# Attention scores built with keys on the partitions, and row maxima entering as a 65th contraction row

## The chip, the core and the metric

One core of one Trainium2 chip runs the whole kernel. The metric is device time in microseconds (us) of one execution; several runs are made and the median is told. The engines are PE (TensorE, matrix products; PEld are its weight loads), DVE (VectorE), ACT (ScalarE), POOL (GpSimd) and SP (SyncE, which here only issues DMAs). Each engine works through its own queue in order; semaphores order the engines among each other. The profile is of one execution.

## The reference

A transformer block on x of shape (4, 2048, 256): causal attention with 4 heads of 64 and rotary embedding, a residual sum and a layer norm; then a mixture of experts with routing, and a second norm. The change lies in the attention alone:

```python
q, k = (_rope(q), _rope(k))
energy = jnp.einsum('bhtd,bhld->bhtl', q, k) + mask
attn = jax.nn.softmax(energy, axis=-1)
out = jnp.einsum('bhtl,bhld->bhtd', attn, v)
out = out.transpose(0, 2, 1, 3).reshape(B, T, D)
return out @ wo.T
```

`mask` is 0 on and below the diagonal and minus infinity above it. q, k and v are x times three 256 x 256 weights; q and k are scaled by 64 to the power -1/4 each.

## The kernel before

`attention` makes normed rows x1 and the first layer of the router (`hidden`) for 64 tiles of 128 tokens (4 sequences of 16 tiles). Three stages follow it and are the same in both kernels: `route`, `experts`, `last_norm`. They start one after the other, each behind a barrier.

Products that need accuracy are made from an upper part (rounded to the type f32r) and a lower part (the rest). For q and k these are in one contraction: `k_st` holds the upper part of k in partitions 0 to 63 and the lower part in 64 to 127, and `q_parts` holds the upper part of q twice and the lower part of q twice, so that two products make one score. Probabilities and v are multiplied as plain f32, which PE issues as two instructions a product.

A *unit* is one tile of 128 queries and one head (256 units); its keys come in *chunks* of up to 512 (640 chunks). For a chunk:

- PE makes the scores with queries on the partitions (L443, two products, and on the diagonal a mask product, L446) into one of 4 banks;
- DVE takes the maximum over the keys (L744, and L748 over a unit's chunks);
- ACT makes exp(score - maximum) and its sum over the keys (L616);
- PE turns the probabilities in blocks of 128 x 128 (L460), so that keys stand on the partitions;
- DVE or ACT copies the turned block (L758, L625; `chunk_owner` says which);
- PE multiplies it with v (L478) into the one bank `out_ps`, which DVE divides by the sums when the tile's four heads are through (L781).

`FIRST` = 20 tiles are projected (L370), rotated (`rope_products` L906, `rope_sums` L912 and L913, on DVE) and turned (L382) ahead of the loop over chunks. The other 44 are projected inside it, four heads at a time, and rotated on POOL. `attention_slots` writes the order out: a list of steps for each chunk number g. Behind a finished tile come its post steps in nine `ROUNDS`, spread over the chunks of the tile after it: turn of the output (`ot`, L509), output projection (`wo`), residual and norm (`ln`, `x1` L809, with one power on POOL, `rstd`, L887), statistics for the router (`stats`, with another power on POOL, L892), turn of x1 (`x1t`, L521) and `hidden` for each second tile. All engines walk the same list (`walk`). `tile_order` puts the short tiles of one sequence between the long ones of the next, and the last sequence's short tiles at the end. On SP's queue stand the loads of x_t (for a tile's projection) and of x rows, and the stores of x1 and of hidden columns.

Of the kernel before, what the change touches and what calls it, by code (L numbers as in the profile page):

```python
# [7 lines left out]
P = 128  # L8
HEADS = 4
HD = 64  # L10
D = 256
# [41 lines left out]
ONE = 1  # L53

AHEAD = 4
PROBS_RING = 8
PT_RING = 4
CH = 512


def raw(ap):
# [4 lines left out]
ROUNDS = (  # L66
    (("qt", 1),),
    (("qt_read", 1), ("kt", 1)),
    (("kt_read", 1), ("proj", 0)),
    (("proj_read", 0), ("ot", 1), ("v", 1)),  # L70
    (("v_read", 1), ("ot_read", 1), ("rope", 0), ("x1t", 2)),
    (("x1t_read", 2), ("wo", 1), ("hidden", 2)),
    (("hidden_read", 2), ("wo_read", 1), ("ln", 1), ("xt", -1)),
    (("x1", 1),),
    (("stats", 1), ("dup", 0)),
)
PROJECTION = ("qt", "kt", "proj", "v", "rope", "xt", "dup")


def tile_order(NB, NT):  # L80

    order = []
    for b in range(NB):
        long = list(reversed(range(4, NT)))
        fill = [(b - 1, t) for t in (3, 2, 1, 0)] if b else []
        for n, t in enumerate(long):
            if n < len(fill):
                order.append(fill[n])
            order.append((b, t))
            if b == NB - 1 and 4 <= n < 8:  # L90
                order.append((b, 7 - n))
    return order


def attention_slots(NB, NT):

    order = tile_order(NB, NT)
    count = len(order)
    units = [(m, h) for m in range(count) for h in range(HEADS)]
    banks = [order[m][1] // 4 + 1 for m, _ in units]  # L100
    chunks = [(u, c) for u, n in enumerate(banks) for c in range(n)]
    start = [sum(banks[:HEADS * m]) for m in range(count + 1)]
    total = len(chunks)

    products, done = [[] for _ in range(total + 2)], 0
    for g in range(total + 2):
        behind = 1 if g >= total or chunks[g][1] in (0, banks[chunks[g][0]] - 1) else 2
        while done < min(g + 1 - behind, total):
            products[g].append(done)
            done += 1  # L110

    span = [(start[m], start[m + 1]) for m in range(count)] + [(total, total + 2)] * 2
    m = 0
    while m < count - 1:
        if order[m][1] < 4 <= order[m + 1][1]:
            half = (start[m] + start[m + 2]) // 2
            span[m], span[m + 1] = (start[m], half), (half, start[m + 2])
            m += 1
        m += 1

    projected = NT + 4
    early, late = ([[] for _ in range(total + 3)] for _ in range(2))
    at, made = 0, {}
    late[0].append(("xt", projected))
    for s in range(count + 2):
        lo, hi = span[s]
        if 1 <= s <= count:
            early[start[s]].append(("sums", s - 1))
            late[start[s]].append(("norm", s - 1))
        for r, steps in enumerate(ROUNDS):  # L130
            offset = r * (hi - lo - 1) // (len(ROUNDS) - 1)
            if r < 3 and s < count and order[s][1] == 3 and order[s][0] < NB - 1:
                offset = 0
            at = min(max(at, lo + offset), total + 2)
            for k, back in steps:
                of = s - back
                if k.removesuffix("_read") in PROJECTION:
                    of += projected
                    if not projected <= of < NB * NT:
                        continue  # L140
                elif not 0 <= of < count:
                    continue
                if k.endswith("_read") and made[k[:-5], of] < at:
                    early[at].append((k, of))
                else:
                    made[k, of] = at
                    late[at].append((k, of))

    for m in range(2, count):
        late[start[m - 1] - 2].append(("q_split", m))  # L150
    return order, units, chunks, banks, products, early, late


def attention(nc, dram, NB, NT):

    order, units, chunks, banks, products_at, early, late = attention_slots(NB, NT)
    CHUNKS = len(chunks)
    first_chunk = np.concatenate([[0], np.cumsum(banks)]).tolist()
    COUNT = NB * NT
    FIRST = NT + 4  # L160
    assert FIRST % 2 == 0 and COUNT % 4 == 0

    def slot(b, t):

        return NT + t if t < 4 and b % 2 else t

    projected = [(n // NT, n % NT) if n < FIRST else
                 (order[n - FIRST][0] + (2 if order[n - FIRST][1] < 4 else 1), order[n - FIRST][1])
                 for n in range(COUNT)]
    nth_projected = {bt: n for n, bt in enumerate(projected)}  # L170
    assert len(nth_projected) == COUNT and max(b for b, _ in projected) == NB - 1

    def cols(b, t):
        return slice(slot(b, t) * P, (slot(b, t) + 1) * P)
# [23 lines left out]
    def walk(main, step):  # L198

        for g in range(len(late)):  # L200
            for kind, k in early[g]:
                step(kind, k)
# [1606 lines left out]
```

## Time and profile before

| | us |
|---|---|
| median of 3 runs | 2280.97 (2280.77 to 2282.14) |
| span of the profiled execution | 2278.6 |
| attention: start to the last product with v | 0 to 1449 |
| post steps of the last tile | 1449 to 1469.5 |
| route, experts, last norm | 1469.5 to 2278.6 |

| engine | busy us | share of the span | instructions |
|---|---|---|---|
| PE | 1967.0 | 86% | 14370 |
| PEld | 1800.5 | 79% | 14370 |
| DVE | 1453.1 | 64% | 3388 |
| ACT | 1361.2 | 60% | 3413 |
| POOL | 805.8 | 35% | 891 |

The span runs from the first to the last instruction on the chip; the page gives no time of its own for this execution, so the span stands beside the median of the runs. PE's busy time counts matmuls that overlap only once, but a matmul's own duration includes its way through the array; what one more matmul costs is therefore read from the start of one to the start of the next. A share of the whole span mixes stages with different limits, so the rows below are taken by stage.

### The profile page before, as it was taken

The numbers are of one execution on the slowest core, as the hardware profiler recorded it, in microseconds if no ns is written. First come the engines' busy times: TensorE is split into PE (matmuls) and PEld (weight loads), VectorE is DVE, ScalarE is ACT, GpSimd is POOL, SyncE is SP. The second block draws the span as 40 slices with busy tenths as digits, with TensorE's granted clock in tenths as the row PEclk, the third lists the DMA queues.
The fourth block names the chain that finished last, engine by engine and source line by source line (L and its number), as shares of the span: only waits on it lengthen the run. The fifth ranks groups of instructions, "written<-read, shape, count | busy, mean of one in ns | idle before, by whom it ended". The sixth has DMA issues, their size and how long they took to land. (4 is left out here: it accounts for less than half of the span.)

```text
span 2278.6 us, 43372 instructions
## 1 busy us (share of the span) xinstructions
PE 1967.0 (86%) x14370; PEld 1800.5 (79%) x14370; DVE 1453.1 (64%) x3388; ACT 1361.2 (60%) x3413; POOL 805.8 (35%) x891
## 2 busy tenths in 40 slices
PE   7899999999999999999999998552177999999990
PEld 6799988888888888888888887451177999999980
DVE  7655676565666666666666676376794566556645
ACT  6666665666666666666566654315175666666655
POOL 2222333323233333233111111100085667666642
PEclk9899999999999999999999999655588999999995
DMA  2000011010001100010000000220004444554428
GB/s 69 21 11 22 22 32 34 22 31 29 27 22 33 32 25 29 23 32 29 20 31 27 24 29 31 78 86 1 0 1 127 148 138 144 162 169 128 149 51 295
DMA packets 91409, 135.85 MB, mean 60 GB/s; under 512 B 16932, under 2 KB 79376, under 8 KB 87148
## 3 DMA queue, kind: packets, MB, share of 16 engines
q1 hardware_dynamic: 75372, 123.52, 15.8%
q0 software_dynamic: 15872, 10.24, 2.7%
q8 instruction: 91, 1.49, 0.3%
q14 instruction: 74, 0.61, 0.1%
HBM read 104.62 MB, written 39.85 MB: 63 GB/s over the span
## 5 line engine op out<-in xcount | busy, mean ns | idle before, releaser
L478 PE MATMUL out_ps<-v_sb,probs_t 128*128 128x64 f32 x4352 | 549.4, 271 | 17.7 <-DVE attn L781 15.2
L478 PEld LDWEIGHTS out_ps<-v_sb,probs_t 128*128 128x128 f32 x4352 | 530.6, 193 | 27.2 <-DVE probs_t L758 20.5
L744 DVE TENSOR_REDUCE part_max<-scores_ps 128x1 f32<-128x512 f32 (+3 forms) x576 | 356.8, 621 | 202.7 <-PE scores_ps L443 148.1
L616 ACT ACTIVATE probs<-scores_ps,neg_max 128x512 f32<-128x512 f32 (+3 forms) x640 | 397.6, 627 | 44.4 <-DVE neg_max L748 42.3
L443 PE MATMUL scores_ps<-k_st,q_parts 128*128 128x512 f32 (+3 forms) x1280 | 410.5, 403 | 11.3 <-ACT probs L616 4.9
L625 ACT COPY probs_t<-probs_t_ps 128x512 f32<-128x512 f32 (+3 forms) x416 | 208.2, 501 | 244.8 <-PE probs_t_ps L460 243.5
L460 PE MATMUL probs_t_ps<-ident,probs 128*128 128x128 f32 x2176 | 347.1, 275 | 1.0 <-DVE probs_t L758 1.0
L460 PEld LDWEIGHTS probs_t_ps<-ident,probs 128*128 128x128 f32 x2176 | 261.4, 142 | 51.2 <-issue 2.4
L1519 PE MATMUL up_ps<-xe_t,w 128*128 128x320 f32 x1920 | 289.2, 310 | 2.2 <-DVE xe_t L1626 1.7
L1519 PEld LDWEIGHTS up_ps<-xe_t,w 128*128 128x128 f32 x1920 | 283.8, 189 | 2.9 <-issue 1.9
L443 PEld LDWEIGHTS scores_ps<-k_st,q_parts 128*128 128x128 f32 x1280 | 200.5, 193 | 25.2 <-ACT probs L616 7.2
L887 POOL TENSOR_TENSOR rstd<-mean_var,power 128x1 f32<-128x1 f32 x64 | 35.6, 556 | 480.0 <-DVE mean_var L801 480.0
L906 POOL TENSOR_TENSOR products<-qk,cos_sin 128x256 f32<-128x256 f32 x176 | 125.4, 744 | 218.3 <-ACT qk L556 218.3
L1640 DVE SCALAR_TENSOR_TENSOR h<-silu,up_ps 128x320 f32<-128x320 f32 x160 | 77.1, 482 | 182.8 <-ACT silu L1596 182.8
L1482 POOL DMA_INDIRECT acc_rows<-out_rows,token x96 | 148.7, 1548 | 127.2 <-ACT out_rows L1609 116.3
L1519 PE MATMUL y_ps<-w,h_parts 128*128 128x256 f32 x1440 | 181.0, 285 | 0.0
L1519 PEld LDWEIGHTS y_ps<-w,h_parts 128*128 128x128 f32 x1440 | 174.4, 191 | 2.2
L1621 DVE TENSOR_TENSOR w<-w_raw,w 128x768 fp32r<-128x768 f32 x160 | 153.0, 958 | 5.0 <-ACT w L1574 1.3
L758 DVE COPY probs_t<-probs_t_ps 128x512 f32<-128x512 f32 (+1 forms) x224 | 145.9, 651 | 0.7 <-PE probs_t_ps L460 0.6
L1462 POOL DMA_INDIRECT rows<-x_rows,token_in x96 | 128.9, 1343 | 48.0 <-POOL token_in L1459 28.4
L1574 ACT CAST w<-w_raw 128x768 fp32r<-128x768 f32 x160 | 131.7, 825 | 8.1 <-PEq L940 8.1
L616 ACT ACTIVATION_READ_ACCUMULATOR probs<-scores_ps,neg_max 128x1 f32 x640 | 130.4, 204 | 0.0
(234 smaller groups left out, 3038.8 us busy)
## 6 DMA issues: line engine op xcount, KB each, us to landing
w_raw<-in_w_expert SPq DMA_DIRECT2D x32, 1536.0 KB
w_raw<-in_w_adapter SPq DMA_DIRECT2D x32, 384.0 KB
x_t<-in_x_t SPq DMA_DIRECT2D x64, 128.0 KB, 2.1
x_row<-in_x SPq DMA_DIRECT2D x64, 128.0 KB, 2.0
x_rows<-x SPq DMA_DIRECT2D x64, 128.0 KB, 1.7
acc_rows<-x SPq DMA_DIRECT2D x64, 128.0 KB, 1.8
ln_x<-acc_rows SPq DMA_DIRECT2D x16, 512.0 KB, 6.3
out_rows_dram<-ln_y SPq DMA_DIRECT2D x16, 512.0 KB, 5.2
```

The source lines that it names most:

```text
L443: mm = pe.matmul(out, q_parts[:, m % 2, part_, h, :], k_st[:, h, key_cols(g)], start=part_ == 0, stop=part_ == 1 and not diagonal)
L460: mm = pe.transpose(t_ps[:, g % 2, a:a + P], probs[:, g % PROBS_RING, a:a + P], ident[:])
L478: mm = pe.matmul(o_ps[:, h, :], probs_t[:, g % PT_RING, a - lo:a - lo + P], v_sb[:, slot(b, a // P), h, :], start=a == 0, stop=a == t * P)
L616: act.activation(probs[:, g % PROBS_RING, 0:hi - lo], s_ps[:, g % AHEAD, 0:hi - lo], ACT.Exp, bias=neg_max[:, u % 8:u % 8 + 1], accum_out= ...
L625: act.copy(probs_t[:, g % PT_RING, 0:hi - lo], t_ps[:, g % 2, 0:hi - lo]).then_inc(probs_copied[1], 1)
L744: red = dve.tensor_reduce(neg_max[:, ring:ring + 1] if single else part_max[:, ring, c:c + 1], s_ps[:, g % AHEAD, 0:hi - lo], AX.X, ALU.ma ...
L758: dve.tensor_copy(probs_t[:, g % PT_RING, 0:hi - lo], t_ps[:, g % 2, 0:hi - lo])\
L1462: pool.indirect_dma_start(out=rows[0:n, r, t, :], out_offset=None, in_=dram["x1"], in_offset=bass.IndirectOffsetOnAxis(ap=token_in[0:n, r, ...
L1482: pool.indirect_dma_start(out=dram["acc"], out_offset=bass.IndirectOffsetOnAxis(ap=token[0:n, r, t:t + 1], axis=0), in_=out[0:n, r, t, :], ...
L1519: mm = pe.matmul(o, left(a), right(b), start=start and n == 0, stop=stop and n == 2)
L1574: act.copy(columns(w[:, r, 0], p), columns(w_raw[:, r], p)).then_inc(w_upper, 1)
L1621: dve.tensor_tensor(columns(w[:, r, 1], p), columns(w_raw[:, r], p), columns(raw(w[:, r, 0]), p), ALU.subtract).then_inc(w_split, 1)
```

## The change

Sequences are worked one after the other, and each in two *phases* of two heads. A unit is now one *group* of four query tiles (512 queries) and one head (64 units), and a chunk is 128 keys against these 512 queries (640 chunks, as before).

- Scores come out with keys on the partitions: the stationary operand is a block of k, the moving one the group's queries (L470, L471). exp of them is the stationary operand of the product with v as it stands (L486), so turns and copies of probabilities are gone.
- The maximum of a query is now needed before the score is built. It is taken from a product of its own, with queries on the partitions and without the lower part of q (L451, one product of up to 512 keys for a query tile; the mask L454; DVE L683). The negative maxima of a unit are turned by PE into a row (L440, four turns of 65 x 128) and copied by DVE into partition 64 of `q_low`, while partition 64 of `k_one` holds ones: the second score product contracts 65 rows, 64 of lower q against upper k and one that subtracts the maximum.
- v has a 65th column of ones, so that the products with v give the sums too (65 columns). `out_ps` has two banks; scores of either kind have two.
- A projection is of two heads (384 columns, L386). 12 of the 128 are made ahead of the loop.
- `Plan` replaces `attention_slots`: one slot for each chunk and 25 more. The post steps of a tile come 8, 5 or 4 slots after those of the tile before it; those of tiles 60 to 63 lie behind the last chunk. The upper half of k is copied once more (`again_k`, POOL).

The core of the diff, with the new order:

```diff
-AHEAD = 4
-PROBS_RING = 8
-PT_RING = 4
...
 CH = 512
+FIRST = 12
+S_AHEAD = 2
+P_RING = 4
...
+class Plan:
...
+        self.groups = [(f, G) for f in range(PH) for G in range(NG)]
+        self.units = [(y, hh) for y in range(len(self.groups)) for hh in range(2)]
+        self.size = [4 * self.groups[y][1] + 4 for y, _ in self.units]
...
+                pace = 8 if self.start[u + 1] < total - per else 5 if self.start[u + 1] < total else 4
+                at = max(at + pace if post else 0, self.start[u + 1] + 1)
...
+            base = 3 * (n - FIRST) if f == 0 else 12 + 4 * t if f == 1 else per * (f - 1) + 5 * t
...
+            late[base].append(("proj", n))
+            early[base + 1].append(("proj_read", n))
+            late[base + 6].append(("kt", n))
...
+                    cur = min(cur - 1, self.start[u] - 6)
...
+            late[at].append(("ot", m))
+            early[at + 1].append(("ot_read", m))
+            late[at + 2].append(("wo", m))
+            early[at + 3].append(("wo_read", m))
+            early[at + 3].append(("ln", m))
+            early[at + 4].append(("x1", m))
+            late[at + 4].append(("stats", m))
+            late[at + 6].append(("x1t", m))
+            early[at + 7].append(("x1t_read", m))
+            late[at + 7].append(("hidden", m))
...
         @block.tensor
...
-                for part_ in range(2):
-                    mm = pe.matmul(out, q_parts[:, m % 2, part_, h, :], k_st[:, h, key_cols(g)],
-                                   start=part_ == 0, stop=part_ == 1 and not diagonal)
...
+            def score(e):
...
+                at_least(pe, score_read, e - 1)
+                if c is None:
+                    pe.wait_ge(neg_ready, u + 1)
+                    for t in range(4):
+                        mm = pe.transpose(out[0:HD + 1, cols(t)], neg_pad[:, u % 2, t, :], ident[:])
...
+                    return
...
+                mm = pe.matmul(out[:, 0:n], q_two[:, ring, hh, cols(i)], k_st[:, h, c * CH:c * CH + n],
+                               start=True, stop=not diagonal)
...
+            def ahead(g):
...
+                at_least(pe, exp_done, g - 1)
+                pe.matmul(out, k_st[:, h, cols(kb)], q_two[:, ring, hh, i * P:CH], start=True, stop=False)
+                mm = pe.matmul(out, k_one[:, h, cols(kb)], q_low[:, ring, hh, i * P:CH], start=False, stop=not diagonal)
...
-                    mm = pe.transpose(t_ps[:, g % 2, a:a + P], probs[:, g % PROBS_RING, a:a + P], ident[:])
...
+                    mm = pe.matmul(o_ps[:, u % 2, t * OS:t * OS + HD + 1], probs[:, g % P_RING, cols(t)],
+                                   v_sb[:, kb, h, 0:HD + 1], start=kb == 0 and t == 0, stop=kb == 4 * G + t,
...
         @block.scalar
...
-                               bias=neg_max[:, u % 8:u % 8 + 1], accum_out=sums[:, m % 2, h, c:c + 1])\
...
+                act.activation(probs[:, g % P_RING, i * P:CH], s_ps[:, g % 2, i * P:CH], ACT.Exp).then_inc(exp_done, 1)
...
         @block.vector
...
+                    dve.tensor_copy(q_low[HD:HD + 1, ring, hh, :], x_ps[HD:HD + 1, e % 2, :]).then_inc(score_read, 1)
...
+                n = (i + 1) * P if c == G else CH
+                dve.tensor_reduce(part_max[:, u % 4, i, c:c + 1], x_ps[:, e % 2, 0:n], AX.X, ALU.max).then_inc(score_read, 1)
+                if e == plan.last_entry[u]:
...
+                    dve.tensor_reduce(neg_pad[:, u % 2, :, HD], part_max[:, u % 4, :, 0:G + 1], AX.X, ALU.max,
+                                      negate=True).then_inc(neg_ready, 1)
```

How the order moves shows at three places. First, PE's queue in the middle of the loop. Before, with `probs_t_ps` the turned probabilities and `out_ps` the products with v (a "128x64" is a product):

```order
L443 MATMUL scores_ps<-k_st,q_parts 128x512 x2
L460 MATMUL probs_t_ps<-ident,probs 128x128 x4
L478 MATMUL out_ps<-v_sb,probs_t 128x64 x8
L443 MATMUL scores_ps<-k_st,q_parts 128x512 x2
L460 MATMUL probs_t_ps<-ident,probs 128x128 x4
```

and now, with `scores_t_ps` the scores with keys on the partitions, `scores_ps` the product for the maxima and `proj_ps` the turned k of a half tile:

```order
L470 MATMUL scores_t_ps<-q_two,k_st 128x512
L471 MATMUL scores_t_ps<-q_low,k_one 128x512
L486 MATMUL out_ps<-v_sb,probs 128x65 x4
L451 MATMUL scores_ps<-k_st,q_two 128x512
L400 MATMUL proj_ps<-ident,k_rows 128x128 x2
```

The four turns of a chunk went, and one product of 512 columns came.

Second, POOL's queue around a post step's power `rstd`. Before:

```order
L906 TENSOR_TENSOR products<-qk,cos_sin 128x256 x4
L912 TENSOR_TENSOR roped<-products 128x8x32
L913 TENSOR_TENSOR roped<-products 128x8x32
L887 TENSOR_TENSOR rstd<-mean_var,power 128x1
L857 TENSOR_TENSOR x_t_parts<-x_t,x_t_parts 128x256
L866 TENSOR_TENSOR q_parts<-q_t,q_parts 128x512
L892 TENSOR_TENSOR x<-powers_of,power 128x2
```

and now, in one alignment of projections and posts (`x<-powers_of` is the second power):

```order
L833 TENSOR_TENSOR products<-qk,cos_sin 128x128 x4
L842 TENSOR_TENSOR q_rows<-products 128x128
L843 TENSOR_TENSOR q_rows<-products 128x128
L842 TENSOR_TENSOR k_rows<-products 128x128
L843 TENSOR_TENSOR k_rows<-products 128x128
L788 COPY k_one<-k_st 64x2x128
L818 TENSOR_TENSOR rstd<-mean_var,power 128x1
L783 TENSOR_TENSOR x_t_parts<-x_t,x_t_parts 128x256
L823 TENSOR_TENSOR x<-powers_of,power 128x2
L833 TENSOR_TENSOR products<-qk,cos_sin 128x128 x4
```

A half tile's rope is eight operations instead of six, and comes every four or five slots; where a post's power falls against it changes from post to post.

Third, the end of PE's queue in this stage, from the last product with v on. Before:

```order
L478 MATMUL out_ps<-v_sb,probs_t 128x64 x5
L509 MATMUL misc_ps<-ident,attn 128x128 x2
L521 MATMUL misc_ps<-ident,x 128x128 x2
L522 MATMUL misc_ps<-ident,x 6x128
L370 MATMUL misc_ps<-w_o,attn_t 128x256 x6
L521 MATMUL misc_ps<-ident,x 128x128 x2
L522 MATMUL misc_ps<-ident,x 6x128
L370 MATMUL misc_ps<-x_t,w_r 128x256 x6
L370 MATMUL misc_ps<-x_ts,w_r1s 128x256 x3
```

and now, the first seven rows:

```order
L486 MATMUL out_ps<-v_sb,probs 128x65 x6
L516 MATMUL misc_ps<-ident,attn 128x128 x2
L386 MATMUL misc_ps<-w_o,attn_t 128x256 x6
L516 MATMUL misc_ps<-ident,attn 128x128 x2
L530 MATMUL misc_ps<-ident,x 128x128 x2
L531 MATMUL misc_ps<-ident,x 6x128
L386 MATMUL misc_ps<-w_o,attn_t 128x256 x6
```

One `ot` (`ident,attn`) stood behind the last product with v, and now there are four.

## Rows read from the trace of the kernel before

**Rows 1.** Busy time by stage; (x) counts instructions, PEclk is the granted clock

```profile
95.00:1400.00 1305.00, 1252.83 (x9599) 1125.05 (x9599) 830.93 (x2135) 831.97 (x2355) 372.06 (x489) 0.99 0.09 27
1400.00:1449.00 49.00, 42.77 (x305) 39.13 (x305) 31.58 (x89) 21.56 (x72) 4.31 (x6) 0.90 0.07 21
```

**Rows 2.** Timeline, PE in steady attention: start us, duration us, instruction

```profile
1003.55 0.62 PE L443 MATMUL scores_ps<-k_st,q_parts 128*128 128x512 f32 x2
1004.01 0.60 PE L460 MATMUL probs_t_ps<-ident,probs 128*128 128x128 f32 x4
1004.45 0.33 PE L478 MATMUL out_ps<-v_sb,probs_t 128*128 128x64 f32 x2
...
1004.85 0.23 PE L446 MATMUL scores_ps<-causal,ident_b 128*128 128x128 bf16 x1
1004.91 0.61 PE L460 MATMUL probs_t_ps<-ident,probs 128*128 128x128 f32 x4
...
1005.50 0.96 PE L370 MATMUL misc_ps<-w_qkv,x_t_parts 128*128 128x256 f32 x6
1006.29 0.63 PE L443 MATMUL scores_ps<-k_st,q_parts 128*128 128x512 f32 x2
```

**Rows 3.** Groups of instructions by line: busy us, mean ns, idle before

```profile
L478 PE MATMUL out_ps<-v_sb,probs_t 128*128 128x64 f32 x4352 | 549.4, 271 | 17.7 <-DVE attn L781 15.2 <-DVE probs_t L758 1.9
...
L744 DVE TENSOR_REDUCE part_max<-scores_ps 128x1 f32<-128x512 f32 x432 | 296.6, 687 | 172.4 <-PE scores_ps L443 148.1 <-PE scores_ps L446 14.1
...
L906 POOL TENSOR_TENSOR products<-qk,cos_sin 128x256 f32<-128x256 f32 x176 | 125.4, 744 | 218.3 <-ACT qk L556 218.3
```

**Rows 4.** Timeline, DVE during the first tiles

```profile
11.95 1.43 DVE L906 TENSOR_TENSOR products<-qk,cos_sin 128x256 f32<-128x256 f32 x4 [0.30 <-ACT qk L592]
...
22.50 1.43 DVE L906 TENSOR_TENSOR products<-qk,cos_sin 128x256 f32<-128x256 f32 x4 [0.34 <-ACT qk L556]
24.02 0.79 DVE L912 TENSOR_TENSOR roped<-products 128x256 f32<-128x256 f32 x1
24.73 0.41 DVE L913 TENSOR_TENSOR roped<-products 128x256 f32<-128x256 f32 x1
25.18 0.69 DVE L717 TENSOR_TENSOR k_st<-probs_t_ps,k_st 64x512 f32 x1
26.17 1.43 DVE L906 TENSOR_TENSOR products<-qk,cos_sin 128x256 f32<-128x256 f32 x4 [0.30 <-ACT qk L556]
```

**Rows 5.** Timeline, PE where the main loop starts

```profile
94.91 1.22 PE L443 MATMUL scores_ps<-k_st,q_parts 128*128 128x512 f32 x2 [1.83 <-ACT probs L616]
```

**Rows 6.** Instructions of L912, ns minimum/median/maximum

```profile
L912 DVE TENSOR_TENSOR roped<-products x20: 425/789/793, 13.5 to 83.2; 128x256 f32<-128x256 f32 x20
```

**Rows 7.** Waits of PE and its weight loads: us, times, longest

```profile
PE out_ps L478 <- DVE attn L781: 15.2, 16, 2.4
...
PEld out_ps L478 <- DVE probs_t L758: 20.5, 26, 2.5
```

**Rows 8.** Timeline, PE after the last attention product

```profile
1447.65 1.33 PE L478 MATMUL out_ps<-v_sb,probs_t 128*128 128x64 f32 x10 [1.15 <-DVE probs_t L758]
1451.05 0.66 PE L509 MATMUL misc_ps<-ident,attn 128*128 128x128 f32 x2 [2.08 <-DVE attn L781]
1452.63 0.69 PE L521 MATMUL misc_ps<-ident,x 128*128 128x128 f32 x2 [0.92 <-DVE attn_t L785]
...
1454.78 1.65 PE L370 MATMUL misc_ps<-w_o,attn_t 128*128 128x256 f32 x6 [1.25 <-DVE x_ts L832]
1461.88 0.66 PE L521 MATMUL misc_ps<-ident,x 128*128 128x128 f32 x2 [5.45 <-POOL x L892]
...
1464.00 1.65 PE L370 MATMUL misc_ps<-x_t,w_r 128*128 128x256 f32 x6 [1.25 <-DVE x_ts L832]
```

**Rows 9.** Timeline, other engines in the same stretch, and the route stage

```profile
1458.57 0.41 DVE L809 TENSOR_SCALAR x<-y,mean_var,rstd 128x256 f32<-128x256 f32 x1 [0.67 <-POOL rstd L887]
...
1469.51 0.20 POOL L1043 MEMSET ident<- 128x128 f32 x1 [7.78 <-POOLq L207]
```

More of the change, by code:

```diff
@@ L77 @@
[L77 to L151, printed above, removed]
@@ L154, in attention @@
-def attention(nc, dram, NB, NT):
[L156 to L174, printed above, removed]
-    owner = [chunk_owner(banks[u], c, u) for u, c in chunks]
-    nth = [owner[:g].count(owner[g]) for g in range(CHUNKS)]
-    copies = [owner.count(e) for e in range(2)]
-    def keys(g):
-        u, c = chunks[g]
-        return c * CH, min((c + 1) * CH, (order[units[u][0]][1] + 1) * P)
-    def key_cols(g):
-        u, c = chunks[g]
-        lo, hi = keys(g)
-        at = slot(order[units[u][0]][0], 4 * c) * P
-        return slice(at, at + hi - lo)
-    def latest_key(g):
-        u, c = chunks[g]
-        b, t = order[units[u][0]]
-        return max(nth_projected[b, x] for x in range(4 * c, min(4 * c + 4, t + 1)))
[L198 to L202, printed above, removed]
-            main(g)
-            for kind, k in late[g]:
-                step(kind, k)
@@ L357, in _ @@
+            for g in range(plan.slots):
+                for kind, k in plan.early[g] + plan.late[g]:
+                    step(kind, k)
             for r in range(2):
@@ L480, in multiply @@
                 mm.then_inc(values_done, 1)
             def main(g):
-                if g + AHEAD < CHUNKS:
-                    scores(g + AHEAD)
+                if g + S_AHEAD < CHUNKS:
+                    ahead(g + S_AHEAD)
                 if g < CHUNKS:
-                    turn(g)
-                for j in products_at[g] if g < CHUNKS + 2 else ():
-                    multiply(j)
+                    multiply(g)
+                for e in plan.score_at[g]:
+                    score(e)
@@ L531, in step @@
                           start=False).then_inc(hid_done, 1)
-            for g in range(AHEAD):
-                scores(g)
-            walk(main, step)
-            while reads:
-                pe.wait_ge(*reads.pop(0))
+            walk(main, step, score, ahead)
+            for bank in pending:
+                pe.wait_ge(*pending[bank])
         @block.scalar
         def _(act):
-            for semaphore in (exp_done, hid_copied, qk_copied, v_copied, q_copied, probs_copied[1]):
-                act.sem_inc(semaphore, ONE)
@@ L877, in step @@
                 elif kind == "proj_read":
[L878 to L884 removed]
+                    pool.wait_ge(qk_copied, k + 1)
@@ L893, in step @@
                         .then_inc(stats_ready, 1)
-            for m in range(2):
-                split_q(m)
-            walk(main, step)
+            walk(nothing, step, nothing, nothing)
 def rope_products(eng, cos_sin, qk, products, t):
```

820 lines of the change are left out of this document (425 added, 395 removed).

## The prediction

> **What bounds the kernel now.** First the busy time by stage [rows 1]: from 95 to 1400 us PE is busy 1252.8 of 1305 us at a granted clock of 0.99, DVE 831, ACT 832, POOL 372. So attention, about 60% of the span, goes by PE's queue. PE's own timeline says what an instruction is worth there, read from start to start, since matmuls overlap [rows 2]: two 512-wide score products 0.46 us (1003.55 to 1004.01), so 0.235 each; four turns of probabilities 0.44, so 0.11 each; a mask 0.06; six 256-wide projection products 0.79, so 0.13 each. Two further stages belong to the change: the first tiles, which end where the main loop's first score starts, at 94.91 [rows 5], and the time from the last attention product (1447.65 + 1.33 = 1448.98) to the start of the route stage at 1469.51 [rows 8, 9]. After that nothing is edited. The sum is made against the profiled execution, span 2278.6; the median of the three runs lies 2.4 above, and I add that at the end. About 0.2%, 4.6 us, is what a measurement can tell from no change.
>
> **PE's exchange in the main loop.** Out go the 2176 turns of probabilities: 2176 x 0.11 = 239 us. In come, by the counts of the two instruction orders:
> - 640 products for the maxima: 448 of 512 columns at 0.235 = 105, and 64 each of 384, 256 and 128 at about 0.14 = 27;
> - a second mask on the diagonal, 256 x 0.06 = 15;
> - the row of negative maxima, 256 turns x 0.11 = 28;
> - projections. Only 12 half tiles instead of 20 whole ones are made ahead of the loop, so 696 products of 384 columns (taken at 0.18, between 0.13 and 0.235) = 125 replace 264 x (0.235 + 0.13) = 97, and there are 120 more turns of q and k, 13. Together 41;
> - less 24 score products that are made ahead of the loop, about 5.
>
> That is 211 in against 239 out: **-28 us**. The pair of score products and the products with v keep their counts. The latter have 65 columns instead of 64: nothing if the weight load sets their pace, at most 1/64 of 549 = 9 us [rows 3]; I take nothing, because an f32 turn of 128 columns has the same 0.11 with one weight load.
>
> The Trainium skill speaks against the size of this term: "TensorE: Matmul & The Clock Gate", section "Back-to-back issue gap", gives sustained spacings of about 81 ns at 128 columns and 131 ns at 512. By these figures (an estimate) the turns are 176 and the 448 wide maxima 59 us, a margin of 117 instead of the 134 of my figures. The rows differ from both figures, and my sum uses the rows.
>
> **Waits that go.** PE waits 15.2 us for the one output bank to be normalised, and its weight loads 20.5 us for copied probabilities [rows 7]. The output bank becomes two and the copy is gone: -36. The last tiles of the order before are short ones: 305 PE instructions take 49 us, at the rate of the main loop 305/9599 x 1305 = 41.5 [rows 1]. The new order ends with its longest units: -7. Together **-43 us**.
>
> **Waits that come.** Maxima now have two score banks, so PE may be two slots (about 2 us each) ahead of DVE. DVE loses the copies of probabilities and gains 64 one-partition row copies and the lower part of q; its 0.69 us maxima stay [rows 3], so it stays near its 64% of this stage and is no bound by itself. What is queued behind what matters more. POOL's rope has eight 128-wide operations per half tile; between half of a 256-wide one and the whole (0.37 to 0.74 [rows 3]) I take 0.5, so 4.0 us every four or five slots. A post step's two powers stand in that queue. When rstd comes right behind a rope (one alignment in five), DVE has x1 up to 3.4 us late; two score banks cover that, but the statistics follow and PE's turn of x1 comes some 1.6 us too early: 64 x 0.3 = 19. Each unit's row needs PE's four turns and a DVE copy of about 0.7 us one slot before its first product: cost between nothing and the whole 1.4, I take 0.3 as DVE has a slot's slack: 19. In the first phase projections come every three slots against some 5.5 us of POOL work: 7. Together **+45 us**, bounds 0 and 64 x (1.6 + 1.4) = 192.
>
> **The first tiles.** DVE sets their pace: 26.17 - 22.50 = 3.67 us a tile, of which its operations fill 1.43 + 0.79 + 0.41 + 0.69 = 3.3 [rows 4]. A half tile has eight rope operations of half the width instead of six. Purely by width a half tile is 1.84 us, by number 3.67; I take 3.0, so 12 take 36 from the same 11.95. Then come setting of the ones row (4096 values in one partition), eight q tiles to turn (1.2 each) and 24 maxima at up to 0.69 with their three rows: 28. The loop starts at 11.95 + 36 + 28 = 76 instead of 94.91: **-19 us** (bounds -41 and -4).
>
> Here a row bears on DVE and POOL working side by side: the rope sums of L912 took 0.425 at the least and 0.789 in the median [rows 6], 0.36 more, where POOL was splitting the next x. I have one such delay in the 3.0. The Trainium skill, "SBUF — State Buffer", section "Who interferes with whom", says that a VectorE instruction with two SBUF inputs and a GpSimd one that reads SBUF lock one port pair, and the loser waits for the whole instruction. That is a rival below.
>
> **The end.** The old order leaves one tile's post work after the last product with v; the new one leaves four (tiles 60 to 63 need both heads of the last unit), four slots apart with nothing between. The old tail shows each link [rows 8, 9]. Last product to the turn of attn 2.07; to PE's next step, which waits for attn's split, 1.58; output projection to x1 1454.78 to 1458.57 = 3.79. So x1 of the first is out 7.4 after the last product. The next one's projection waits in PE's queue behind this one's turn of x1 (3.31 after x1) and its split (1461.88 to 1464.00 = 2.12), so the period is 3.31 + 2.12 + 3.79 = 9.2. Three periods, then x1 to the route stage 10.94: 7.4 + 27.7 + 10.9 = 46 against 20.5 now: **+26 us**.
>
> **At no cost.** ACT loses the accumulator reads and its copies of probabilities and gains smaller reads; it is 64% busy in the loop and exp has two slots of lead. x_t is loaded 128 times instead of 64, each two projections (at least six slots) ahead on SP's queue; x rows, stores and hidden columns follow the plan's slots there, behind signals that are due by then. If that cover went, each late load would cost PE its 2 us or so.
>
> **Sum.** -28 - 43 + 45 - 19 + 26 = -19: 2259.6 for the profile, with 2.4 on it **2262 us**, a ratio of 0.992. Its own range, from the bounds of the start and half the bounds of the waits, is 2235 to 2276.
>
> **Rivals.**
> 1. **Posts wait in POOL's queue, and PE with them** (slower). DVE stands at x1 while rstd is behind rope; maxima stand behind DVE; PE reaches its third maximum, or the turn of x1, and stops. For: POOL goes from 372 to some 690 us of this stage, with rope right ahead of rstd in its order. Against: two slots of lead, and DVE idle for a third of the time. Price: if every post loses the 1.6 that I gave to the worst alignment, 64 x 1.6 = 102 in place of 19: 2345 us. It decides from 0.6 us a post on.
> 2. **The waits are hidden** (faster still). All chains fit in their two slots: the 45 goes, 2217 us. For it speaks that plan slots are two steps apart for each step of a chain; against it, that the old order has 36 us of waits of just this kind.
> 3. **The port** (no change). If the loser waits a whole POOL instruction of 0.73 at both POOL operations of a half tile, the start is 12 x (1.46 - 0.36) = 13 longer, and x1 of every fifth post reaches PE later by as much, some 4: 2279 us. For: 0.789 against 0.425. Against: the 0.36 is half an instruction.
>
> **How the numbers follow.** My forecast 0.42, rival 1 0.29, rival 2 0.22, rival 3 0.07. Faster is the forecast and rival 2, 0.64; no change rival 3, 0.07; slower rival 1, 0.29. The range 2200 to 2335 takes in rival 2 with room for a quicker start, and rival 1 up to 1.4 us a post; the rest of rival 1, about a tenth, is left out above, and somewhat less below.
>
> **What would show it.** The main loop's first score at about 76; 640 products for the maxima at a start-to-start of 0.235; the time from there to the last product with v near 1328 us (1354 - 28 - 43 + 45); POOL about half busy there; rstd waiting on POOL in one post of five; 46 us from the last product to the route stage. Wrong would be: PE waiting hundreds of times for a score bank or for DVE's row; a products-with-v group that grew by more than 9 us; a start later than 91; a lower granted clock in the loop.

## The result, and the profile after

The change makes the kernel slower: median 2341.19 us of 4 runs (2327.95 to 2351.55) against 2280.87 for the kernel before, a ratio of 1.026 (95% interval 1.023 to 1.029). The forecast was 2262, the range 2200 to 2335. Runs differ with the mean granted clock: the shortest of the changed kernel, 2328 us, had 0.888, its two longest, 2350.5 and 2351.6, had 0.878 and 0.879, and one run of e9 below, at 0.633, took 2737 us against 2197 to 2199 for its other five. The profiled execution is one of the long ones, with a span of 2348.7.

First the busy time by stage, for the kernel before and after, from the main loop's start (its first score before, its first product with v after) to the last product with v. Columns: stretch, its length, busy time and instructions of PE, PEld, DVE, ACT and POOL, granted clock, DMA share, GB/s.

Before:

```profile
94.90:1449.00 1354.10, 1295.69 (x9904) 1164.28 (x9904) 862.51 (x2223) 853.63 (x2427) 376.37 (x495) 0.99 0.09 26
```

After, the loop and then the lowest two and the highest of six stretches of 200 us in it, which answer to [rows 1]:

```profile
83.80:1494.60 1410.80, 1353.86 (x9085) 1215.09 (x9084) 801.67 (x2003) 610.06 (x1610) 593.75 (x1278) 0.93 0.10 31
...
200.00:400.00 200.00, 193.62 (x1260) 174.31 (x1260) 110.24 (x270) 85.00 (x223) 87.84 (x191) 0.89 0.10 29
...
800.00:1000.00 200.00, 194.36 (x1335) 174.70 (x1334) 117.41 (x289) 89.56 (x238) 95.24 (x206) 0.95 0.11 32
...
1200.00:1400.00 200.00, 193.01 (x1241) 172.20 (x1240) 112.75 (x286) 82.54 (x213) 64.25 (x137) 0.88 0.09 27
```

PE has 819 instructions fewer in the loop and is busy 58 us longer. Its pauses, the time in which it is not busy, are the same in sum: 1354.1 - 1295.7 = 58 us before, 1410.8 - 1353.9 = 57 after. But 28 of them are over a microsecond now, 39.9 us together, and 12 were before, 19.9 us. The other difference is the clock column: 0.99 before, 0.93 after, and in the stretches 0.88 to 0.95. By the clock's own record in the trace, 207 us of this loop ran at 1.2 GHz, the lower of its two levels, against 32 us before. At half the clock PE does about half the work (an instruction of the products with v takes 200 ns from start to start in those stretches, and 103 ns at the higher level), so about half of that time is lost: 103 us against 16. So **some 87 us** of the loop are the clock. Without pauses and without that half, PE's work is 1354.1 - 58.4 - 15.9 = 1280 us before and 1410.8 - 56.9 - 103.3 = 1251 after. That the exchange of work did save PE some 29 us can be read here and nowhere in the total.

Where does the clock fall? One case in the changed kernel: the timelines of DVE and POOL and then of PE (start us, duration us, instruction, and in brackets the idle time before it and who ended that), and the busy time by stretch around it.

```profile
320.53 0.18 DVE L730 BATCH_NORM_AGGREGATE mean_var<-moments 128x2 f32<-128x6 f32 x1
320.79 0.15 DVE L732 TENSOR_SCALAR mean_var<-mean_var 128x1 f32<-128x1 f32 x1
...
321.06 0.46 POOL L842 TENSOR_TENSOR q_rows<-products 128x128 f32<-128x128 f32 x1
...
322.30 0.46 POOL L843 TENSOR_TENSOR k_rows<-products 128x128 f32<-128x128 f32 x1
...
322.72 0.55 POOL L818 TENSOR_TENSOR rstd<-mean_var,power 128x1 f32<-128x1 f32 x1
```

```profile
324.00 0.48 PE L451 MATMUL scores_ps<-k_st,q_two 128*128 128x512 f32 x1
324.31 0.40 PE L470 MATMUL scores_t_ps<-q_two,k_st 128*128 128x512 f32 x1
324.55 0.39 PE L471 MATMUL scores_t_ps<-q_low,k_one 65*128 65x512 f32 x1
324.78 1.00 PE L486 MATMUL out_ps<-v_sb,probs 128*128 128x65 f32 x8
...
327.26 0.41 PE L530 MATMUL misc_ps<-ident,x 128*128 128x128 f32 x2 [1.29 <-POOL x L823]
```

```profile
310.00:325.00 15.00, 15.00 (x109) 13.83 (x107) 10.13 (x25) 7.50 (x21) 9.43 (x21) 1.00 0.07 19
325.00:328.00 3.00, 1.71 (x15) 1.53 (x14) 1.98 (x8) 1.08 (x4) 1.38 (x2) 1.00 0.00 0
328.00:340.00 12.00, 12.00 (x48) 10.44 (x47) 2.45 (x6) 3.36 (x10) 3.80 (x9) 0.50 0.14 44
340.00:355.00 15.00, 15.00 (x63) 13.80 (x63) 6.77 (x18) 3.22 (x10) 1.31 (x3) 0.50 0.12 36
355.00:370.00 15.00, 15.00 (x106) 13.85 (x104) 9.41 (x21) 8.20 (x21) 10.14 (x22) 0.99 0.07 19
```

`mean_var` is ready at 320.94; `rstd` stands behind a rope in POOL's queue until 322.72, 1.8 us later. x1 is late by it, and PE pauses 1.29 us at its turn of x1 (L530). At 328 the clock falls to half and stays there for 27 us, in which PE never waits: 48 matmuls in 12 us at half the clock, 106 in 15 us after it. Each of the 15 falls in this loop comes 1.3 to 3.5 us after the beginning of such a pause, of 1.15 to 2.03 us; a stretch at half clock lasts 3 to 27 us. The other 13 pauses over a microsecond brought no fall, and the length of a pause does not set what it costs: the six of 1.29 or 1.30 us at L530 were followed by 20 to 27 us at half clock each, 143 in all, and the three of 2.02 or 2.03 us there by none, 3 and 7.

The waits of PE from 90 to 1495 us (us in all, times, longest):

```profile
PE misc_ps L530 <- POOL x L823: 19.8, 20, 2.0
PE proj_ps L400 <- POOL k_rows L843: 13.1, 9, 1.7
PE misc_ps L530 <- DVE attn_t L719: 6.0, 8, 1.2
PE scores_ps L451 <- DVE part_max L683: 3.7, 4, 1.2
PE proj_ps L386 <- DVE k_st L652: 3.0, 3, 1.0
PE scores_ps L451 <- DVE q_low L680: 2.8, 5, 0.6
```

Two kinds of pause are the longest, L530 and L400. The second is named after the wrong engine. The timeline at one of them:

```profile
284.83 0.15 DVE L756 TENSOR_SCALAR powers_of<-x 128x1 f32<-128x1 f32 x1
285.02 0.43 DVE L652 TENSOR_TENSOR k_st<-proj_ps,k_st 64x256 fp32r<-64x256 f32 x1
...
285.50 0.20 PEld L400 LDWEIGHTS proj_ps<-ident,q_rows 128*128 128x128 f32 x2 [1.96 <-DVE k_st L652]
285.50 0.44 PE L400 MATMUL proj_ps<-ident,q_rows 128*128 128x128 f32 x2 [1.66 <-POOL k_rows L843]
```

PE wants to turn q into the bank `proj_ps`, where the k turned one slot earlier still waits for DVE: the lower part of k (L652) stood behind the six statistics of a post step. POOL's `k_rows` ended by chance at the same time; the weight load's row has the right name.

### The profile page after: what moved, and what is told of

Its sections match the earlier page's. It is cut to its first block and busy times, and to the rows that moved or that the text cites. A ratio compares the mean times of both kernels' runs of the same rounds, so it can differ in the third digit from the quotient of the medians.

```text
span 2348.7 us, 40554 instructions
## 1 busy us (share of the span) xinstructions
PE 2013.2 (86%) x13346; PEld 1833.9 (78%) x13346; DVE 1393.7 (59%) x3208; ACT 1084.1 (46%) x2549; POOL 1022.5 (44%) x1683
## 5 line engine op out<-in xcount | busy, mean ns | idle before, releaser
L486 PEld LDWEIGHTS out_ps<-v_sb,probs 128*128 128x128 f32 x4352 | 607.6, 204 | 35.9
L683 DVE TENSOR_REDUCE part_max<-scores_ps 128x1 f32<-128x512 f32 (+3 forms) x640 | 388.5, 609 | 388.8 <-PE scores_ps L454 231.2
L486 PE MATMUL out_ps<-v_sb,probs 128*128 128x65 f32 x4352 | 605.1, 281 | 0.0
L582 ACT ACTIVATE probs<-scores_t_ps 128x512 f32<-128x512 f32 (+3 forms) x640 | 340.9, 533 | 324.1 <-PE scores_t_ps L473 183.7
L833 POOL TENSOR_TENSOR products<-qk,cos_sin 128x128 f32<-128x128 f32 x464 | 199.9, 461 | 382.6 <-ACT qk L559 342.4
L451 PE MATMUL scores_ps<-k_st,q_two 128*128 128x512 f32 (+3 forms) x640 | 298.1, 468 | 9.8 <-DVE part_max L683 4.3
L470 PE MATMUL scores_t_ps<-q_two,k_st 128*128 128x512 f32 (+3 forms) x640 | 272.5, 426 | 0.0
L471 PE MATMUL scores_t_ps<-q_low,k_one 65*128 65x512 f32 (+3 forms) x640 | 245.1, 383 | 0.0
L386 PE MATMUL proj_ps<-w_qkv,x_t_parts 128*128 128x384 f32 x696 | 158.7, 367 | 3.8 <-DVE k_st L652 3.0
L451 PEld LDWEIGHTS scores_ps<-k_st,q_two 128*128 128x128 f32 x640 | 130.7, 205 | 16.7 <-DVE part_max L683 8.4
L386 PEld LDWEIGHTS proj_ps<-w_qkv,x_t_parts 128*128 128x128 f32 x696 | 133.8, 206 | 8.8 <-DVE k_st L652 3.7
```

The costliest lines, as they stand in the source:

```text
L386: mm = pe.matmul(out, parts_l(a), parts_r(b), start=start and n == 0, stop=stop and n == 2)
L451: mm = pe.matmul(out[:, 0:n], q_two[:, ring, hh, cols(i)], k_st[:, h, c * CH:c * CH + n], start=True, stop=not diagonal)
L470: pe.matmul(out, k_st[:, h, cols(kb)], q_two[:, ring, hh, i * P:CH], start=True, stop=False)
L471: mm = pe.matmul(out, k_one[:, h, cols(kb)], q_low[:, ring, hh, i * P:CH], start=False, stop=not diagonal)
L486: mm = pe.matmul(o_ps[:, u % 2, t * OS:t * OS + HD + 1], probs[:, g % P_RING, cols(t)], v_sb[:, kb, h, 0:HD + 1], start=kb == 0 and t == 0 ...
L582: act.activation(probs[:, g % P_RING, i * P:CH], s_ps[:, g % 2, i * P:CH], ACT.Exp).then_inc(exp_done, 1)
```

## The experiments

Theory A: PE's pauses of over a microsecond are what the falls of the clock follow, so they cost several times their length. Rival B: waits cost only themselves, and the clock goes its own way. Theory C: the product for the maxima is dearer than I took it, for its place ahead of two other f32r products. Each run was timed against the kernel before on the same chip. The columns on the right are of the profiled execution: the loop's length (first to last product with v; before, from the loop's first score), PE's pauses in it, time at half clock in it, and length - pauses - half of the half-clock time. Counted from its first product with v too, the kernel before has 1349.7, 58, 27 and 1278.

| kernel | median us | ratio to before, 95% | span | loop | pauses | half clock | rest |
|---|---|---|---|---|---|---|---|
| before | 2280.9 | | 2278.6 | 1354.1 | 58 | 32 | 1280 |
| the change | 2341.2 | 1.023 to 1.029 | 2348.7 | 1410.8 | 57 | 207 | 1251 |
| e1_rope_after | 2256.7 | 0.987 to 0.990 | 2255.5 | 1316.4 | 41 | 28 | 1262 |
| e2_rope_before | 2406.9 | 1.053 to 1.060 | 2396.0 | 1458.8 | 112 | 181 | 1256 |
| e3_kt_later | 2295.2 | 1.002 to 1.008 | 2280.3 | 1343.0 | 67 | 28 | 1262 |
| e4_between | 2266.4 | 0.992 to 0.995 | 2263.8 | 1326.4 | 49 | 56 | 1249 |
| e5_filler | 2276.8 | 0.997 to 1.001 | 2304.5 | 1364.8 | 43 | 102 | 1271 |
| e6_lag | 2235.2 | 0.979 to 0.983 | 2231.2 | 1293.8 | 32 | 6 | 1259 |
| e7_lag_between | 2230.8 | 0.976 to 0.985 | 2216.2 | 1280.0 | 27 | 4 | 1251 |
| e8_tail | 2213.1 | 0.969 to 0.978 | 2211.6 | 1283.8 | 27 | 11 | 1251 |
| e9_xt_early | 2197.9 | 0.963 to 0.965 | 2195.4 | 1267.0 | 17 | 5 | 1248 |
| e10_half_maxima | 2172.3 | 0.951 to 0.954 | 2169.1 | 1242.4 | 29 | 4 | 1212 |

The last column is 1248 to 1262 us for every kernel that does just the work of the change (e5 does 141 instructions more, and e10 leaves out some). Pauses and clock are the rest.

**Order on POOL.** Projections every fourth slot instead of every fifth keep a fixed place to the posts, which come every eighth. With + 1 each rope stands behind a post's two powers:

```diff
-ROW_RING = 12
+ROW_RING = 16
-            base = 3 * (n - FIRST) if f == 0 else 12 + 4 * t if f == 1 else per * (f - 1) + 5 * t
+            base = 3 * (n - FIRST) if f == 0 else 12 + 4 * t if f == 1 else per * (f - 1) + 4 * t + 1
...
```

> Projections every fourth slot, placed so that POOL's rope always stands behind a post step's two powers; 16 row buffers instead of 12, nothing else. Theory A (a pause of PE of more than about a microsecond is followed by a stretch at half clock): the 19.8 us of PE waiting at its turn of x1 fall below 5, the half-clock time in the loop falls from about 200 us to below 90, and the time from 2341 to about 2341 - 18 - 55 = 2268. Rival B (the clock goes its own way, waits cost only themselves): half-clock time stays near 200 us and the time falls by the waits alone, to about 2322.

Measured 2256.7, 84 us less than the change and 24 less than before. In the loop the waits at the turn of x1 are 11.6 us instead of 19.8 (up to 1.5 each; more than the 5 expected), the half-clock time 28 us instead of 207. This speaks for theory A; rival B's 2322 is 65 us off. The waits at L400 went as well, from 16.1 us by all that ended them to 1.5, so the turn of x1 is not all that the new order eased.

With + 3 in place of + 1, and nothing else changed against e1, a rope stands right ahead of `rstd`:

```diff
-            base = 3 * (n - FIRST) if f == 0 else 12 + 4 * t if f == 1 else per * (f - 1) + 4 * t + 1
+            base = 3 * (n - FIRST) if f == 0 else 12 + 4 * t if f == 1 else per * (f - 1) + 4 * t + 3
```

> The same kernel as the one with rope behind the powers, but with projections two slots later, so that a rope always stands right ahead of rstd in POOL's queue. Theory A: nearly every post with rope beside it makes PE wait about a microsecond at its turn of x1, some 50 us in all, and half-clock time in the loop grows to over 300 us: 2341 + 30 + 50 = about 2420. Rival B: the waits alone, about 2370, and the half-clock time as before.

Measured 2406.9: nearly A's time, but not in A's way. The waits of PE from 84 to 1543 us:

```profile
PE proj_ps L400 <- DVE k_st L652: 43.4, 16, 4.0
PE proj_ps L386 <- DVE k_st L652: 31.8, 21, 2.1
...
PE misc_ps L530 <- POOL x L823: 8.1, 8, 1.5
```

The late posts show at the bank `proj_ps`, because the lower part of k stands behind them on DVE. Half-clock time did not grow to 300; it is 181 us, in 27 stretches instead of 15, half as long on average, and here B's "as before" was nearer. Against the change 55 us more are pauses (112 - 57) and 13 less the clock. So this run tells that the order on POOL sets the pauses, and not how much clock a pause costs.

**The bank of k and q.**

```diff
-            late[base + 6].append(("kt", n))
-            early[base + 7].append(("kt_read", n))
+            turn = base + (6 if f == 0 else 7 if f == 1 else 8)
+            late[turn].append(("kt", n))
+            early[turn + 1].append(("kt_read", n))
...
```

> PE's turn of k one or two slots later, nothing else. Theory A: the 13.1 us that PE waits for k_rows at L400 go, and with them the six falls of the clock behind such a wait (41 us at half clock): 2341 - 13 - 20 = about 2308. The falls behind the turn of x1 stay. Rival B: -13, about 2328.

Measured 2295.2 (2282 to 2316; the profiled execution is one of the shorter ones), 46 us less where A said 33, and my reading was wrong on two points. What waits at L400 is the turn of q, and for DVE (above). And the pauses did not get less: 67 us, 30 of them over a microsecond, 39.0 us together (28 and 39.9 in the change), yet the clock fell only three times, each behind a pause of 2.44 us, and half of the half-clock time is 14 us instead of 103. The waits at the turn of x1 were left as they were, and here one of 1.25 us passed with no fall (busy time by stretch, this kernel):

```profile
300.00:318.00 18.00, 18.00 (x129) 16.46 (x128) 12.44 (x32) 8.73 (x26) 9.15 (x20) 1.00 0.11 35
318.00:322.00 4.00, 2.75 (x24) 2.50 (x23) 2.98 (x11) 2.09 (x6) 1.73 (x3) 1.00 0.06 17
322.00:340.00 18.00, 17.21 (x123) 15.31 (x123) 10.40 (x26) 7.98 (x22) 7.92 (x18) 1.00 0.18 56
```

So a pause is what a fall follows, but not every pause has one. Which ones do stays open.

**The place of the product for the maxima.**

```diff
                 for t in range(i, 4):
+                    if t > i and rest:
+                        score(rest.pop(0))
...
```

> The product for the maxima is put between two products with v instead of right ahead of the next pair of score products. Theory C (an f32r product of 512 columns takes 0.315 us to the next f32r product but 0.234 to an f32 one): PE saves up to 0.08 us for each of 640 products, 35 to 50 us, about 2298, with the clock as it was. Rival: the 0.08 only moves to another place, 2341 within 8.

Measured 2266.4, 75 us less, but theory C is wrong. PE in that kernel:

```profile
333.97 0.33 PE L489 MATMUL out_ps<-v_sb,probs 128*128 128x65 f32 x2
334.11 0.48 PE L451 MATMUL scores_ps<-k_st,q_two 128*128 128x512 f32 x1
334.43 0.33 PE L489 MATMUL out_ps<-v_sb,probs 128*128 128x65 f32 x2
```

From 334.11 to 334.43 it is 0.32 us, with a plain f32 product behind it, as it was 0.31 ahead of an f32r one (324.00 to 324.31 above). The work of the loop is the same, 1249 against 1251. The loop of the profiled execution is 84 us shorter: 75 is half of the 151 us less at half clock, and 8 are pauses. Why this order, with 25 pauses over a microsecond, has fewer falls (7) stays open as well.

**Useless work in the pauses.** The sharpest test of A leaves every wait in place and fills the twelve longest at the turn of x1:

```diff
+LATE = dict.fromkeys((3, 13, 16, 19, 29, 35, 45, 48, 52), 10) | dict.fromkeys((8, 24, 40), 17)
...
                     claim("b", x1_split, k + 1)
+                    for _ in range(LATE.get(k, 0)):
+                        pe.transpose(b_ps[:, 3 * P:4 * P], ident[:], ident[:])
                     pe.wait_ge(stats_ready, k + 1)
```

> The changed kernel with useless work added: ahead of the twelve turns of x1 at which PE paused over a microsecond, 10 or 17 turns of the identity into a free part of the bank (1.1 or 1.9 us). Nothing arrives earlier, PE's waits are only filled. Theory A (it is PE's pause that the half clock follows): the eight falls behind such a pause, 154 us at half clock, go, and the kernel is faster by up to 77 us for 141 more instructions: about 2270. Rival B (waits cost themselves, the clock goes its own way): 2341 or up to 5 more.

Measured 2276.8: 141 instructions more, and 64 us less, near A's 2270 and far from B's 2341. PE, and the busy time by stretch, at the post shown above:

```profile
325.91 1.26 PE L530 MATMUL misc_ps<-ident 128*128 128x128 f32 x10
327.27 0.44 PE L533 MATMUL misc_ps<-ident,x 128*128 128x128 f32 x2
```

```profile
324.00:328.00 4.00, 3.90 (x31) 3.47 (x31) 3.08 (x10) 2.15 (x7) 1.39 (x2) 1.00 0.00 0
328.00:340.00 12.00, 12.00 (x92) 10.76 (x90) 5.37 (x14) 4.83 (x13) 4.83 (x11) 1.00 0.17 56
340.00:355.00 15.00, 14.52 (x102) 13.26 (x101) 10.72 (x26) 7.76 (x21) 8.18 (x19) 1.00 0.12 36
```

The turn of x1 comes at 327.27 as it came at 327.26, and the clock stays: 92 matmuls from 328 to 340 us instead of 48. All eight falls behind the turn of x1 are gone. Five others remain, each behind a pause of 1.65 to 2.01 us at L400, which was not filled; a sixth came at 1403 behind three pauses of 0.34 to 0.46. The profiled execution, 2306 us, is the longest of this kernel's eleven: there the clock then stayed at half to the end of the loop.

**Taking the pauses away.**

```diff
-            late[at + 6].append(("x1t", m))
-            late[at + 7].append(("hidden", m))
+            late[at + 6 + lag[m]].append(("x1t", m))
+            late[at + 7 + 2 * lag[m]].append(("hidden", m))
...
```

`lag` is 1 for posts eight slots apart, else 0; the reads follow; the rest is as in the kernel with rope behind the powers.

> As the kernel with rope behind the powers, and PE's turn of x1 one slot later, hidden two. If the remaining 27 us of waits at that turn (some 15 in the loop, the rest in the tail) and the three falls behind them (24 us at half clock) cost what they seem to: 2257 - 10 - 12 = about 2235. If the waits only move to hidden or to the next turn of attn: 2257.

Measured 2235.2. No fall in the loop at all, though 15 pauses of over a microsecond are left, 17.5 us together.

> The same with the product for the maxima put between two products with v. Its start-to-start stayed 0.314 us there, so what it brought before was the clock (207 us at half clock before, 56 with it). If that is so, little is left to bring here: 0 to 13 us faster than the kernel without it, 2222 to 2235. If it saves PE time of its own, 40 or more: below 2200.

Measured 2230.8 (2218.0 to 2240.7; the profiled execution is the shortest), which can't be told from e6. With the clock up, the place of the product brings next to nothing, as it should if its gain was the clock.

The last four posts two slots apart:

```diff
-                pace = 8 if self.start[u + 1] < total - per else 5 if self.start[u + 1] < total else 4
+                pace = 8 if self.start[u + 1] < total - per else 5 if self.start[u + 1] < total else 2
```

> The same, and the last four post steps two slots apart instead of four, so that PE makes the next tile's output projection before this one's turn of x1. The tail from the last product with v to the route stage, 45 us, has three periods of 9.2 us; if DVE's chain of about 6.5 us is what is left of a period, 8 us faster than the kernel without it; if steps of neighbouring tiles get in each other's way, the same or slower.

Measured 2213.1 (2210.6 to 2232.5). PE's last products with v and the route stage's first row:

```profile
1366.30 1.50 PE L490 MATMUL out_ps<-v_sb,probs 128*128 128x65 f32 x12
...
1402.34 0.21 POOL L971 MEMSET ident<- 128x128 f32 x1 [7.77 <-POOLq L222]
```

1402.34 - 1367.80 = 34.5 us; e7 and the change both have 44.3 (the change's rows stand below): 10 less in the tail. The medians differ by 18, but the runs of both spread by 22, so the tail's 10 is what the profile shows.

```diff
-                late[max(base - 2, 0)].append(("xt", n))
+                late[max(base - (4 if f > 1 else 2), 0)].append(("xt", n))
```

> As the kernel with the shorter tail, and POOL splits the next x two slots earlier, ahead of the rope that it now stands behind. The 10.8 us in 16 waits of PE for that split go: about 2203 against 2213. If the split, earlier, pushes rope and the powers back by as much as it gains: 2213.

Measured 2197.9: **3.6% faster than the kernel before and 6.1% faster than the change**, with the same arithmetic. Its pauses are 17 us instead of 27 and the wait for the split is gone:

```profile
83.70:1350.70 1267.00, 1249.78 (x9085) 1132.52 (x9084) 790.93 (x2003) 610.18 (x1610) 597.27 (x1278) 1.00 0.11 35
```

**The price of a product for the maxima.**

```diff
-                n = (i + 1) * P if diagonal else CH
+                n = (i + 1) * P if diagonal else CH // 2
...
```

> The kernel with the shorter tail, with 384 of the 640 products for the maxima (those of whole key chunks) over half their keys, and DVE's maxima of them too: half of those chunks is left out of the maximum. If a product for the maxima costs PE what the trace shows from start to start, 0.33 us at 512 columns and 0.21 at 256: 384 x 0.12 = 46 us less, 2167. If it costs the 0.235 and 0.14 of the prediction: 384 x 0.095 = 36 less, 2177. If PE is no longer what bounds the loop: nothing.

Measured 2172.3, 41 less than e8; the loop's rest falls by 39 (1251 to 1212). Halving 384 products took off 0.10 us each, between the 0.095 of my prices and the 0.12 of the trace. Of the full 0.32, then, about 0.1 does not go with the columns.

## Why the prediction was wrong

The stages of the profiled executions add up: 11 us less ahead of the loop, 57 more in it, 24 more behind it and 0.5 in the stages that were not edited are 70, and the spans differ by 2348.7 - 2278.6 = 70. By the prediction's own steps, with the loop's parts summed from the start of one matmul to the start of the next and pauses left out:

- **PE's exchange, -28: right, by misses that nearly cancel.** The rest column gives 1251 - 1280 = -29 (-21 in e6, whose loop is at full clock). In e6 the products for the maxima are 0.33, 0.26, 0.21 and 0.15 us at 512, 384, 256 and 128 columns: 448 x 0.33 + 64 x 0.62 = 188 us instead of 132, 56 too few. The turns that go were 242 (239 taken). On the other side the products with v took 450 us against 464 before although they have 65 columns; the pair of score products 287 against 301 (5 fewer taken), the rows 22 (28 taken), projections of every kind with the turns of q and k 260 against 230 (41 more taken). Together these turn -28 into some -15, 6 short of e6's -21. The margin of turns over wide maxima is 242 - 148 = 94. My rows gave 134. The estimate by the Trainium skill, "TensorE: Matmul & The Clock Gate", section "Back-to-back issue gap", gave 117, nearer, but from 81 and 131 ns, where the traces have 111 and 330.
- **Waits, -43 + 45: right in sum, and partly by luck.** Pauses 58 before, 57 after. The 19 us at the turn of x1 are 19.8, by the mechanism that was named (`rstd` behind rope, PE 1.3 us too early in the post above), but in 20 posts, by 1.0 us on average and 2.0 at most, instead of 1.6 in one post of five. The 19 for the rows were 2.8 and the 7 of the first phase 3.0; not foreseen were 16.1 at L400 (13.1 in the row above for `k_rows`). On the other side, the 20.5 us that were to go with the copies of probabilities are waits of weight loads [rows 7]; PE's own for those copies were 2.9 (1.9 at the products with v, 1.0 at the turns).
- **The first tiles, -19: -12.** The loop's first score stands at 83.13 (76 forecast, 94.91 before [rows 5]). The half tiles came every 2.9 us (12.02 to 44.21 for eleven) as taken (3.0); what follows them, from 47 us on, took 36 instead of 28, with the clock at half from 35 to 89 us. DVE's first and last of the twelve, and PE:

```profile
12.02 1.43 DVE L833 TENSOR_TENSOR products<-qk,cos_sin 128x128 f32<-128x128 f32 x4 [2.86 <-ACT qk L559]
...
44.21 0.90 DVE L833 TENSOR_TENSOR products<-qk,cos_sin 128x128 f32<-128x128 f32 x4
...
83.13 0.56 PE L470 MATMUL scores_t_ps<-q_two,k_st 128*128 128x256 f32 x1
```

- **The end, +26: +24.** From the last product with v (1493.31 + 1.50) to the route stage 44.3 us, 46 forecast, 20.5 before [rows 8, 9], with the period of 9.2 between turns of x1:

```profile
1493.31 1.50 PE L486 MATMUL out_ps<-v_sb,probs 128*128 128x65 f32 x12
...
1503.41 0.66 PE L530 MATMUL misc_ps<-ident,x 128*128 128x128 f32 x2 [4.47 <-POOL x L823]
...
1512.63 0.66 PE L530 MATMUL misc_ps<-ident,x 128*128 128x128 f32 x2 [4.24 <-POOL x L823]
...
1539.10 0.20 POOL L967 MEMSET ident<- 128x128 f32 x1 [7.79 <-POOLq L221]
```

- **The step that failed is one that isn't there: the clock.** Each term was priced at the 0.99 of [rows 1], and the 45 us of new waits at their own length. The pauses have the same sum as before, but 28 instead of 12 are over a microsecond: before, 0.99 of the clock with 58 us of pauses; now 0.93 with 57. That is the missing 87 us: 1328 forecast for the loop plus 87 is 1415, measured 1411. "A lower granted clock in the loop" stood in the list of what would make the prediction wrong, with no price and no chance. Filled pauses (e5), pauses taken away (e1, e6) and the sum in the last column show that it is the cause. Which pauses bring a fall, and for how long, they do not show.
- **Rival 1** gave 2345 and the kernel takes 2341, but that is no hit for its price. Its mechanism, posts waiting in POOL's queue, is there; it was to cost 102 us of PE's waits, and they are 20. The rest is the clock behind them. Rival 2's hidden waits are what e9 comes near to: with pauses of 17 us in its loop that kernel takes 2198, 10 of it by the shorter tail, where rival 2 gave 2217.
- **Rival 3, the port,** did not come at its price. In the first tiles L842, which takes DVE 0.28 us alone, took 0.87 and 0.86 where POOL's split of the next x began 0.01 or 0.02 us ahead of it:

```profile
15.96 0.73 POOL L783 TENSOR_TENSOR x_t_parts<-x_t,x_t_parts 128x256 fp32r<-128x256 f32 x1 [0.84 <-ACT x_t_parts L553]
15.97 0.87 DVE L842 TENSOR_TENSOR q_rows<-products 128x128 f32<-128x128 f32 x1
...
17.16 0.28 DVE L842 TENSOR_TENSOR k_rows<-products 128x128 f32<-128x128 f32 x1
```

So a wait for a whole operation of POOL happens, but the rope operations of the twelve half tiles took some 6 us longer beside POOL in all, where the forecast had 12 x 0.36 = 4.3 and the rival 12 x 1.46 = 17.5.
- **The range called its own, 2235 to 2276,** does not follow from the bounds that the prediction names: -41 and -4 around the start's -19, and half of the waits' 0 to 192 around their 45, give 2195 to 2328, near the 2200 to 2335 that was put down. No working is shown for -41 and -4; 1.84 and 3.67 us a half tile alone give -33 and -11.
- **DVE and the score banks**, which the prediction spared, were rightly spared: PE waits 3.7 us for DVE's maxima. POOL is busy 42% of the loop (593.8 of 1410.8), about the half that was taken, its rope 0.46 us an operation instead of 0.5.

## What to carry to other kernels

Where PE bounds a stage, look for the places where it pauses for a microsecond or more, and do not price them at their length alone: here 28 of them, 40 us together, had 103 us of lost clock behind them. That is no fixed rate (30 of them, 39 us, had 14 in e3), so give the granted clock a term, a bound and a chance of its own in the forecast. Moving three steps of an order table by a slot or two was worth more than the whole exchange of work. Give steps of different periods a fixed place to each other (every fourth beside every eighth, not every fifth), so that one engine's long job never comes right ahead of a short one that PE waits for. If a pause can't be removed, work of no use in it can pay (e5: 64 us).

## What the runs showed of the hardware

- In a loop where PE is busy for 96% of the time, 15 of its 28 pauses over a microsecond, of 1.15 to 2.03 us, were each followed by 3 to 27 us at 1.2 GHz, in the case shown with PE busy all the while. The Trainium skill, "TensorE: Matmul & The Clock Gate", section "A second HAM failure mode: psum-queue depth-cycling", tells of a kernel whose clock swings because PE idles briefly and often between groups of matmuls; this case agrees in that the clock swings, here behind single pauses, and e5 shows it by filling them. Much the same pause brought a fall in one order and none in another (1.29 us in the change, 1.25 in e3; 15 over a microsecond in e6 without one), and at one place of one order (2.03 us at L530 in the change, once with a fall and once without). What decides was not settled.
- A product with 65 columns beside an f32 weight load of 128 x 128 is no dearer than one with 64: 103 ns from start to start against 107.
- An f32r product of 512 columns took 0.31 to 0.33 us where it was made for the maxima, in two places of the order, and 0.23 as the second of a pair with 65 contraction rows (324.55 to 324.78). Why these differ was not tried.
